# A slot network's first weights, slot preparation and first four tiles, made inside the attention stage before it

## The reference

```
x = x + attn_a(layernorm(x))        # 16 heads, windows of 1024 queries, causal
x = x + slots(layernorm(x))         # "the first network"
x = x + attn_b(layernorm(x))        # a gated linear recurrence
x = x + slots(layernorm(x))         # "the second network", same weights
```

```
S = slot_init                                   # 64 x 1024
ctx = concat([x, mean(S)], -1)
h = gelu(ctx @ w1 + b1)                         # w1: 2048 x 512
logits = (h @ w2 + b2) / (|tau| + 0.1)          # 64 slots
alpha = softmax over the 8 largest of 64, zero elsewhere
si = (alpha^T x) / sum(alpha)                   # 64 x 1024
gi = si @ Wih.T + bih ; gh = S @ Whh.T + bhh    # gates of a GRU cell
S_new = gru(gi, gh, S), then attention among slots, layernorm, two products
out = alpha @ slot_values @ wo + bo
```

## Time and profile before

| | |
|---|---|
| median of 3 runs | 2324.51 us (2321.56 to 2467.65) |
| profiled execution | 2319.89 us |
| its span, slowest core | 2318.4 us |
| spans of the eight cores | 2309.5 to 2318.4 us |
| PE busy, mean granted clock | 1797.7 us (78%), 0.882 |
| DVE, ACT, POOL busy | 1389.2, 1077.2, 823.5 us |
| chain that ended last | PE 50%, DVE 14%, POOL 11%, issue 10%, ACT 8%, DMA 5% |

### The profile page before, as it was taken

One profiled execution on the slowest core, in us unless ns is written; L12 is line 12 of the kernel. 1 busy time (PEld: TensorE's weight loads), 2 busy tenths in 40 slices (PEclk: granted clock), 3 DMA queues, 4 the chain that ended last, 5 costly groups with the idle time before them and its releaser, 6 DMA issues.

```text
span 2318.4 us, 43243 instructions; the slowest of 8 cores (2309.5 to 2318.4 us)
## 1 busy us (share of the span) xinstructions
PE 1797.7 (78%) x14810; PEld 997.9 (43%) x14810; DVE 1389.2 (60%) x2326; ACT 1077.2 (46%) x1704; POOL 823.5 (36%) x693
## 2 busy tenths in 40 slices
PE   4979999999837863468888888888888888757756
PEld 2434444444413432235455555555555555423331
DVE  5355646554335643666677776766667776547646
ACT  0057575766514431155555555555555555425510
POOL 2000000000021101356566776666666776421100
PEclk9989999999868886689899999999999999879975
DMA  9312413212299989220221112221221111189879
GB/s 212 62 38 92 126 65 108 77 66 85 79 200 215 224 140 176 72 92 29 73 74 61 51 65 74 74 73 48 73 74 65 60 60 38 37 195 224 174 259 335
DMA packets 92583, 251.65 MB, mean 109 GB/s; under 512 B 13232, under 2 KB 21425, under 8 KB 92372
## 3 DMA queue, kind: packets, MB, share of 16 engines
q1 hardware_dynamic: 51876, 178.98, 23.5%
q0 software_dynamic: 35888, 53.13, 15.4%
q10 hardware_dynamic: 4608, 16.78, 2.1%
HBM read 234.10 MB, written 67.90 MB: 130 GB/s over the span
## 4 chain that ended last, share of the span: by engine, by line
PE 50%; DVE 14%; POOL 11%; issue 10%; ACT 8%; DMA 5%; DVEq 0%; SPq 0%; ACTq 0%; POOLq 0%
PE bF L1819 11%; PE aF L411 6%; PE aF L429 5%; PE aS L463 3%; PE aO L444 3%; PE bF L1829 3%; ACT Wslot L486 3%; PE bF L1933 2%; POOL xout L1722 2%; POOL xout L1726 2%; PE f_F L909 2%; POOL htok L2378 2%; DVE b_m L2200 2%; POOL b_xx L2342 1%; PE aF L419 1%
## 5 line engine op out<-in xcount | busy, mean ns | idle before, releaser
L486 ACT ACTIVATE Wslot<-aS,cvals_s 128x1024 bf16<-128x1024 f32 (+3 forms) x384 | 328.4, 900 | 175.6 <-PE aS L463 174.7
L1819 PE MATMUL bF<-xout,Wslot 128*128 128x256 bf16 x2048 | 271.4, 292 | 21.4 <-ACT hfeat L2048 8.3
L1722 POOL TENSOR_TENSOR xout<-b_m,b_hf 128x1024 bf16<-128x1024 bf16 x128 | 250.2, 1966 | 83.7 <-DVE b_m L2200 83.6
L1819 PEld LDWEIGHTS bF<-xout,Wslot 128*128 128x128 bf16 x2048 | 205.5, 104 | 83.5 <-issue 46.7
L2200 DVE TENSOR_TENSOR b_m<-bB,b_xx 128x1024 bf16<-128x1024 f32 x128 | 155.3, 1215 | 50.8 <-PE bB L1781 49.0
L617 POOL TENSOR_SCALAR ave<-amv 128x1 f32<-128x1 f32 x32 | 8.3, 261 | 451.5 <-DVE amv L499 451.5
L463 PE MATMUL aS<-aQf,aKf 64*128 64x512 bf16 (+3 forms) x768 | 137.2, 353 | 23.6 <-ACT Wslot L486 17.3
L444 PE MATMUL aO<-aVaug,Wslot 128*128 128x65 bf16 x2304 | 131.9, 200 | 24.5 <-DVE Wslot L551 24.1
L2367 POOL TENSOR_TENSOR b_rk<-hfeat 128x1024 bf16<-128x1024 bf16 x32 | 69.9, 2186 | 195.9 <-ACT hfeat L2048 195.9
L2048 ACT ACTIVATE hfeat<-bF 128x512 bf16<-128x512 f32 x128 | 76.2, 595 | 136.1 <-PE bF L1819 135.9
L1933 PE MATMUL bF<-Wslot,b_ygT 128*128 128x512 bf16 x512 | 129.6, 399 | 4.8 <-ACT b_vt L2055 4.6
(11 more groups left out here) (307 smaller groups left out, 3842.3 us busy)
## 6 DMA issues: line engine op xcount, KB each, us to landing
xin<-x1d SPq DMA_DIRECT2D x64, 512.0 KB, 7.9
xin<-x3d SPq DMA_DIRECT2D x38, 512.0 KB, 8.6
xin<-x SPq DMA_DIRECT2D x32, 512.0 KB, 5.0
xout<-x SPq DMA_DIRECT2D x32, 512.0 KB, 4.3
x1d<-xout SPq DMA_DIRECT2D x32, 512.0 KB, 3.1
x2d<-xin SPq DMA_DIRECT2D x32, 512.0 KB, 2.6
xin<-x2d SPq DMA_DIRECT2D x32, 512.0 KB, 3.2
x3d<-xin SPq DMA_DIRECT2D x32, 512.0 KB, 4.0
```

Source lines behind the costliest of these rows:

```text
L486: e_ex.inc(a.activation(Pk[:, :, qo:512], psS[i % 2][:, :, 0:512 - qo], AF.Exp, bias=cvals[:, 1:2], scale=0.125), s)
L1722: return eng.tensor_tensor(dst, mm[:].rearrange("p (a o q) -> p a o q", a=2, o=2), hf[n % 2][:, 2 * s:2 * s + 2, :].unsqueeze(1).broadcast_to(
L1819: mm = t.matmul(ps[:, o * 256:(o + 1) * 256], w[:, dc, oc * 128:(oc + 1) * 128], mixb[:, sl, dc, :], start=(dc == 0), stop=(dc == NDC - 1))
```

## The change

The order of each network's DVE work is changed in both networks: LS of the next tile comes before LN of the one before. Everything else concerns the first network's start, which moves into attention A:

- w1a and w1b are loaded into W[0] by POOL after Q(7,7), in the last block of attention A; slots and w2 right after the attention's own weights; b1, b2, tau and the ones by SP after its first loads.
- The slot preparation becomes three fillers of the last block, in its pair 5: PT (transposes), PS (mean and 1/tau), PB (w1b). |tau| is made on DVE instead of ACT, at the first step of the last block, ahead of its mask.
- Tiles 0 to 3 of the attention's own result are loaded, normalised in pairs 0 to 3 of the last block, and stay in `htok`; tiles 4 to 7 are loaded behind them. The first network leaves out LS, LR and LN of tiles 0 to 3 and the loads of tiles 0 to 7.

```diff
+class Ahead:
+    def __init__(self, ctx, stack, slot):
...
+        w = slot[:].rearrange("p a b -> p (a b)")
+        self.w1a = w[:, 0:4096].rearrange("p (a o) -> p a o", o=512)
+        self.w1b = w[:, 4096:8192].rearrange("p (a o) -> p a o", o=512)
...
-                return [None] * 3 + ot + wo
+                return [None] * 3 + ot + wo + [("PT",), ("PS",), ("PB",)]
...
+        for t in range(BT):
+            lns_st[(NBLK - 1, t, 0)] = 32 + t
+            lns_nm[(NBLK - 1, t, 3)] = 32 + t
...
+                elif kind == "PT":
+                    nx.e["s"].wait_ge(t, 0)
+                    pst = ps[:].bitcast(BF16)
+                    for dc in range(NDC):
+                        mm = t.transpose(pst[:, dc * 64:(dc + 1) * 64],
+                                         S0b[:, dc * 128:(dc + 1) * 128],
+                                         identb[0:64, 0:64])
+                elif kind == "PS":
+                    for dc in range(NDC):
+                        t.matmul(ps[:, dc:dc + 1], S0b[:, dc * 128:(dc + 1) * 128],
+                                 onesb[0:64, 0:1], start=True, stop=True)
+                    nx.v.wait_ge(t, "tau")
+                    mm = t.matmul(ps[:, 8:9], nx.onesf[:], nx.tau[0:1, 2:3],
+                                  start=True, stop=True)
+                elif kind == "PB":
+                    e_fe.wait_ge(t, ("PS",))
+                    nx.e["w1b"].wait_ge(t, 0)
+                    for oc in range(4):
+                        for dc in range(NDC):
+                            mm = t.matmul(ps[:, oc:oc + 1],
+                                          nx.w1b[:, dc, oc * 128:(oc + 1) * 128],
+                                          nx.smb[:, dc:dc + 1],
+                                          start=(dc == 0), stop=(dc == NDC - 1))
...
+                if s == (NBLK - 1, 0, 0):
+                    nx.e["b"].wait_ge(v, 3)
+                    nx.v.inc(v.scalar_tensor_tensor(
+                        nx.tau[0:1, 1:2], nx.tau[0:1, 0:1], -1.0,
+                        nx.tau[0:1, 0:1], ALU.mult, ALU.max), "abs")
...
+            nx.e["s"].inc(gp.dma_start(out=S0b[:], in_=dram["fslot"][:, :]), 0)
+            nx.e["w2"].inc(gp.dma_start(
+                out=nx.w2[:], in_=dram["fw2"].rearrange("(oc p) s -> p oc s", p=128)),
+                0)
             gp.memset(mhalf[:], -0.5)
-            for g in range(32):
+            for g in range(36):
+                if g == 32:
+                    e_fill.wait_ge(gp, ("Q", NBLK - 1, 7))
+                    for key, dst in (("w1b", nx.w1b), ("w1a", nx.w1a)):
+                        nx.e[key].inc(gp.dma_start(
+                            out=dst, in_=dram["f" + key].rearrange(
+                                "(dc p) o -> p dc o", p=128)), 0)
...
+                else:
+                    nx.x[g % 4].inc(s_.dma_start(
+                        out=xin[:, g % 4, :],
+                        in_=x_out[(g - 32) * 128:(g - 31) * 128, :]), g - 32)
...
-                if s in lns_nm and lns_nm[s] + 4 < 32:
+                if s in lns_nm:
                     ldx(lns_nm[s] + 4)
...
                 ("GM", b, 0), ("LS", n[0]), ("LR", n[0]), ("TA", b - 1),
-                ("GM", b, 1), ("LN", n[0]), ("LS", n[1]), ("LR", n[1]),
+                ("LS", n[1]),
+                ("GM", b, 1), ("LN", n[0]), ("LR", n[1]),
                 ("EX", b - 1),
                 ("LT", n[0]),
-                ("GM", b, 2), ("TB", b - 1), ("LN", n[1]), ("LS", n[2]),
+                ("GM", b, 2), ("TB", b - 1), ("LS", n[2]), ("LN", n[1]),
                 ("LR", n[2]),
                 ("LT", n[1]),
-                ("GM", b, 3), ("LN", n[2]), ("LS", n[3]), ("LR", n[3]),
+                ("GM", b, 3), ("LS", n[3]), ("LN", n[2]), ("LR", n[3]),
                 ("LT", n[2]), ("LN", n[3]),
...
+                if first and t[0] in ("LS", "LR", "LN") and t[1] < 4:
+                    continue
...
-                    d_["LN"].wait_ge(t, ("LN", g))
+                    if not first or g >= 4:
+                        d_["LN"].wait_ge(t, ("LN", g))
...
-                        if b == 0:
+                        if b == 0 and first:
+                            nx.e["w1a"].wait_ge(t, 0)
+                            nx.e["w2"].wait_ge(t, 0)
+                        elif b == 0:
                             e_w["1"].wait_ge(t, 1)
...
-            if first:
-                pre_p.wait_ge(gp, "b1")
```

More of the change, by code:

```diff
@@ L221, in closed @@
         assert self.n == len(self.keys), (self.sem, self.n, len(self.keys))
+class Ahead:
+    def __init__(self, ctx, stack, slot):
+        sb = lambda n, shp, dt: ctx.sb("n_" + n, shp, dt, stack=stack)
+        self.w2 = sb("w2", (128, 4, 64), BF16)
+        self.sT = sb("sT", (128, 8, 64), BF16)
+        self.smb = sb("smb", (128, 8), BF16)
+        self.b1t = sb("b1t", (128, 4), F32)
+        self.tau = sb("tau", (1, 4), F32)
+        self.onesf = sb("onesf", (1, 128), F32)
+        w = slot[:].rearrange("p a b -> p (a b)")
+        self.w1a = w[:, 0:4096].rearrange("p (a o) -> p a o", o=512)
+        self.w1b = w[:, 4096:8192].rearrange("p (a o) -> p a o", o=512)
+        self.e = {k: Ev(ctx, "n_" + k, range(n), 16)
+                  for k, n in (("s", 1), ("w2", 1), ("w1a", 1), ("w1b", 1), ("b", 4))}
+        self.x = [Ev(ctx, f"n_x{i}", range(i, 8, 4), 16) for i in range(4)]
+        self.v = Ev(ctx, "n_v", ["abs", "tau0", "tau", "stau", "b2"])
 def build(nc, sh):
@@ L673, in emit_attn_a, with emit_ffn @@
         asc.close()
[L675 removed]
+    def emit_ffn(x_in, x_out, tag, first, bw_pre=None, nx=None):
         fsc = contextlib.ExitStack()
@@ L787, in emit_ffn @@
         e_rc = ev("rc", of("TB"))
-        e_x = [ev(f"x{i}", range(i, 32, 4), 16) for i in range(4)]
+        e_x = [ev(f"x{i}", range(i + 8 * first, 32, 4), 16) for i in range(4)]
         if not first:
@@ L1121, in dve @@
                     g = tok[1]
-                    e_x[g % 4].wait_ge(v, g)
+                    if first and g < 8:
+                        nx.x[g % 4].wait_ge(v, g)
+                    else:
+                        e_x[g % 4].wait_ge(v, g)
                     x = xt[g % 4]
@@ L1290, in rows @@
                 return src.rearrange("(dc p) o -> p dc o", p=128)
-            if first:
-                e_0["s"].inc(gp.dma_start(out=S0b[:], in_=dram["fslot"][:, :]), 0)
-                e_0["w1b"].inc(gp.dma_start(out=w1b, in_=rows(dram["fw1b"])), 0)
-            e_w["1"].inc(gp.dma_start(out=w1a, in_=rows(dram["fw1a"])), 0)
-            e_w["1"].inc(gp.dma_start(
-                out=w2[:], in_=dram["fw2"].rearrange("(oc p) s -> p oc s", p=128)), 1)
-            if first:
+            if not first:
+                e_w["1"].inc(gp.dma_start(out=w1a, in_=rows(dram["fw1a"])), 0)
+                e_w["1"].inc(gp.dma_start(
+                    out=w2[:],
+                    in_=dram["fw2"].rearrange("(oc p) s -> p oc s", p=128)), 1)
+            else:
                 e_0["bh"].inc(gp.dma_start(out=bhb[:, 0:3072], in_=dram["fbhh"][:, :]), 0)
@@ L1351, in ldx @@
                                             in_=x_in[g * 128:(g + 1) * 128, :]), g)
[L1353 to L1360 removed]
+            if not first:
+                for g in range(4):
+                    ldx(g)
             e_w["b"].inc(s_.dma_start(out=bq[:, 0:2], in_=dram["fbq"][:, :]), 0)
```

124 lines of the change are left out of this document (47 added, 77 removed).

## The result

The changed kernel takes 2299.2 us in the median of 16 runs (2294.5 to 2414.7) against 2322.8 for the kernel before on the same chip. In some executions of any kernel here the cores of one or both dies show a lower granted clock and the time is some per cent longer (up to 2414.7 above), so each ratio compares the other executions alone. It is 0.9904 (95% interval 0.9885 to 0.9923): 18 to 27 us faster, inside the 2% called "same". The forecast was 2297 in a range of 2281 to 2312. The profiled execution took 2294.96 us, and its span went from 2318.4 to 2293.4. The slowest core is number 6 now and was number 2, so I also give means over the eight cores of one profiled execution (us). "Start" runs from a network's first POOL instruction to GM(0,0), "blocks" from there to the first product with Wih; attention A counts from 0.

A forecast was written before the change was run, and what follows sets the result against it. Bound: an unhidden w1b load at the first network's start, then PE and DVE taking turns. Terms -33.9 + 4.2 + 5.4 - 4.1 + 2.0 = -26.4 turn 2319.9 into 2293.5 us, 2297 against the median; range 2281 to 2312.

The forecast's parts named there:

- part 3: Steady blocks of both networks: statistics ahead of normalisation bring LT(n1) 1.5 us later; +4.2 us first network, +5.4 second.
- Part 1: First network's start: loads, slot preparation and four tiles' work removed, GM(1,0) at 663.2 instead of 697.13: -33.9 us.
- Part 2: First network's DMA queue: 27.2 us of loads leave, Wih still lands in time with 6 us margin: 0 us.
- full-rate case: Steady blocks, if GM(b,3) takes 1.89 us instead of 3.11: the new order gives -0.2 us per block; chance 14%.
- Part 4: Second network's start and block 0: GM(0,0) 2.4 us sooner, then held by w2's load; GM(1,0) sooner by 4.1: -4.1 us.
- Part 5: Last block of attention A: PE's extra work in pair 5 +1.4 us, operations on tau +0.6: +2.0 us.
- Rival D: Last attention block: the added work is paid in full, 12.7 us instead of 2.0, giving 2308 us; chance 7%.
- A: First network: the loads bind it, Wih landing 6.8 us after it is wanted, giving 2304 us; chance 13%.
- B: Steady blocks: the order costs nothing, GM(b,3) at full rate, -0.2 us in each of eleven blocks, 2284 us; chance 14%.
- C: Steady blocks: longer idle before LT(n1) keeps PE at the low clock, some 7.4 us a block, 2367 us; chance 4%.

The follow-up runs named there:

- extra load: The changed kernel with wv loaded a second time (2 MB) ahead of the second part of Wih; ratio 0.9921 to the kernel before.
- half loads: The changed kernel with each network's own x loads bringing only 512 of a tile's 1024 columns; ratio 0.9866 to the kernel before.
- order alone: The kernel before with only the new order, LS of the next tile ahead of LN, in both networks; ratio 1.0026 to the kernel before.
- tiles back: The changed kernel with tiles 0 to 3 still loaded in the attention stage but normalised in the first network; ratio 0.9963 to the kernel before.
- LR first: The changed kernel with POOL's first LRs ahead of the late weight loads, and w2 ahead of w1a in the second network; ratio 0.9900 to the kernel before.
- attention clean: The changed kernel with slots', w2's and small loads issued later and 1/tau made behind the first step's mask; ratio 0.9892 to the kernel before.
- mixed order: The changed kernel with the old order from block 1 on, except LS of the fourth tile ahead of LN of the third; ratio 0.9827 to the kernel before.

## Why the prediction was right, and where it was not

The time was right, and the first part carried it. Smaller terms were wrong in size and cancelled, which is luck: the order cost 5.8 us less than forecast (part 3), and the head, the second start and block 0 behind it gained 4.8 less.

**Part 1, the head: right.** Forecast -33.9 to GM(1,0); the eight cores' mean is 38.2 + 14.2 before and 6.8 + 13.1 after, -32.5. LT(0), the table load and GM(0,0) came as computed, and LN(4) behind POOL too. I had put DVE's chain behind that wait 1 us short of PE's path; with LN(7) 2.0 sooner GM(1,0) stayed, so PE's own work sets it.

**Part 2, the queue: right, with less room.** The mid phase is unchanged (53.7, 53.5). The forecast margin was 6 us; from the extra load I estimate 4 to 5. It was consumed at once when another 7 us left the stage.

**Part 3, the order: right in the mechanism, wrong in the size.** LT(n1) comes 10.21 after the block's start where it came at 8.65, 1.6 later for the 1.5 forecast. I priced every steady block at +0.9 to +1.0 by one row with a slow GM(b,3), and gave the full-rate case -0.2 as a rival. Both happen in the same kernel, block by block: 17.1 (-0.5) and about 18.9 (+1.2). The mean of 48 blocks is +0.16 where +0.9 was forecast: +1.0 for blocks 1 to 6 of the second network instead of +5.4. In the first network GM(1,0) to the gate products went from 151.9 to 154.7, +2.8 for a forecast of +4.2, and with other parts. Block 1 became 1.2 shorter (forecast +1.0), block 3 did not change (+1.5), block 4 became 1.4 longer (+1.5), block 5 did not change and block 6 became 1.3 longer (+1.0 each). Block 2, forecast -1.8, went up by 1.6: DVE's waits for the bias loads grew from 11.4 to 13.5 in the cores' mean, where I had them shrink (core 6, DVE, for the 10.17 of the earlier trace rows):

```profile
710.80 0.68 DVE L1248 TENSOR_TENSOR aT<-f_F,aT 64x512 f32<-64x512 f32 x1 [12.34 <-DMA aT<-fbihc]
```

The step that failed is the one from a single row to a count: the earlier trace rows were one of 48 blocks. 38 of them had the slow last GM, and 25 with the new order, not all.

**Part 4, the second start: the direction right, the size not.** Forecast -4.1, measured -1.5 at GM(0,0), and block 0, forecast -1.7, took 0.8 more instead. The mean hides two cases. On four cores GM(0,0) came at 19.7 after the stage's begin and waited for LT(3)'s eviction alone: 4.4 sooner than the 24.2 of most cores before, near the 4.8 I had for DVE's part. On the other four it waited for w2 until 26.1 to 27.1. The landing of w2 at 20.2 us was one core's; over the cores and kernels here GM(0,0) comes between 19.7 and 29.7 us. With half loads it came at 19.7 on all eight cores and never waited for w2, so what held it is the competition of x and the weights for the DMA engines, which the order of LS and LN does not touch.

**Part 5, the last attention block: too dear.** Forecast +2.0. From the first to the last mask its eight pairs took 70.61 us before and 70.22 after (means of the cores). Pair 0 went from 7.64 to 7.08, since the operations on tau now delay the mask that it is counted from (the pair before grew by 0.6, as forecast): with those 0.56 added back the block pays 0.2. Pair 5 went from 7.33 to 7.70: PT, PS and PB cost 0.4 there, not 1.4. Rival D is out.

**Rivals.** A false as long as nothing else shortens the stage, and true one step later. B true in 23 of the second network's 48 blocks, more strongly than I had it. C false: the clock is back with the next work, as the earlier trace rows said.

## What to carry to other kernels

A wait that a slow matmul hides behind is slack; before spending it, read how many of the repeats already need it, not one of them. When a stage's compute gets shorter, look in the same trace at the margin of its next load, since the order of a queue decides then; here a gain of 7 us in the blocks came back as 7.9 us in the mid phase, and moving two loads won 6.0 of them again. The longest wait named at a new start need not be the path; take it away before building on it, and look in that run's trace whether it has gone or only moved, as from LN(4) to LN(6) here.

## What the hardware showed that I had not expected

Behind the idle time ahead of LT(n1) the granted clock over the next 3.7 us was sometimes 1.00 and sometimes 0.50 to 0.68, in blocks with the same instructions. In seven kernels with the new order and the gap left open (the changed one, order alone, tiles back, LR first, attention clean, half loads, extra load) 193 of 336 blocks of the second network were long and every one of them had the slow last GM, and none of the 143 short ones. The length of the gap alone does not decide it: between 3.2 and 3.9 us, where 279 of the 336 lie, 152 were slow and 127 were not, while all 29 gaps of 4.0 or more were slow; and before and with the mixed order, with gaps of 2.9 to 3.2, 77 of 96 were slow. The place counts more: with the new order 189 of 224 blocks 1 to 4 were slow and 4 of 112 blocks 5 and 6. No run here shows why.

And an x load of 256 KB took 9.4 us to land beside a full weights' queue, as long as one of 512 KB (9.7), but 2.6 us once that queue was empty. The Trainium skill, "DMA: Bandwidth & Descriptors", section "Queues, rings and completion order", says that each DMA engine takes turns between queues packet by packet. The equal landing times agree with that, and so do the plain queue's 990 and 1018 packets in the same 30 us, with 3.60 and 1.86 MB; no run here separates it from other causes.
